# Scores for the maxima of attention: from six products of parts in one set of TensorE's rows to three products in two sets

## The chip, the cores and the metric

The kernel runs on one core of a Trainium2 chip. A core has TensorE (PE; its weight loads are shown as PEld), VectorE (DVE), ScalarE (ACT), GpSimd (POOL) and SyncE (SP), which only issues transfers here. The metric is the device time of one execution in microseconds, taken as the median of the runs.

## What is computed

One pre-norm transformer layer on x of shape (2, 2048, 256), in float32. The attention has 16 heads of 16 features, with rotation by position and a causal mask:

```python
q, k = (rope(q), rope(k))
att = jnp.einsum('bhqd,bhkd->bhqk', q, k) / scale
att = jnp.where(mask, att, -jnp.inf)
att = jax.nn.softmax(att, axis=-1)
y = jnp.einsum('bhqk,bhkd->bhqd', att, v)
```

The feed-forward part has 704 inner features; each of its three products takes both operands rounded blockwise (16 numbers share a scale) to the FP4 grid and scaled back:

```python
gate = fp4_linear(x, w_gate)
y = fp4_linear(x, w_up)
h = jax.nn.silu(gate) * y
return fp4_linear(h, w_down)
```

Each half is x plus its result on the normalised x.

## The kernel before, in words

**Tiling.** The 4096 rows are 8 chunks of 512 queries (four for each of the two sequences), and the heads are four groups of four. A chunk and a group make a unit: 32 units (`units`), worked in order. c is the number of chunks before the unit's own in its sequence, 0 to 3.

**Parts.** q and k are split into three bf16 numbers each (high, middle, low), stored to `parts_dram`, and dealt from there by SyncE into `q_mem` and `k_mem` (`deal`, L804 to L826, three DMAs each for q and k of a unit). The dealing lays the parts above each other in the rows (partitions) so that one product over 96 rows, `TERM_ROWS`, adds six products of parts of 16 features: float32 accuracy from bf16. Three more rows of q hold the negative maximum in parts and meet ones in k.

**Maxima.** For a stable softmax each query's largest score is found first (`maxima`, L864 to L879 on TensorE, L1268 to L1283 on VectorE). A piece is 32 queries of the four heads by 512 keys: four matmuls, each over 96 rows into its own 32 columns of the array, side by side, fill one bank of PSUM. VectorE takes the maximum of each row: of past keys by a reduction (L1282), of the unit's own chunk by an operation that adds the triangular mask and takes the maximum (L1279, shown as a custom operation and a read of the accumulator). Own blocks have 32, 64, ... 512 keys, two in a bank where they fit. In all there are 1056 pieces (768 of them past), at most `S_IN_FLIGHT` = 3 undrained.

**Placing.** After the last piece of a unit VectorE forms the negative maxima in three parts and turns them; three DMAs (`place_maxima`, L725 to L732) put them into rows of `q_mem`, by ScalarE's queue for the first two chunks and by SyncE's later.

**Probabilities.** For each of a unit's key tiles (128 keys) and each head, four matmuls of 32 keys each (L896, rows 0 to 98) give scores less the maximum; at the diagonal four more add the mask (L901). ScalarE takes the exponential into `prob` (L1177). Then four float32 matmuls, one a head, add prob times V to bank 7 (`values`, L920; each is recorded as two).

**The rest.** Projections (L966 to L999), a tile's feed-forward part in units of 128 queries (L927 to L1044), normalising (L1006) and the weights' turning use the whole array. Rounding to the grid takes six steps on VectorE and three on GpSimd (`quantise`, L1492 to L1505): add, subtract, and multiply by the scale, each on the whole row of 256 or 704 numbers.

**Order.** A planner at the head of `preln_layer` (`Plan`, `rehearse_...`) rehearses all jobs with assumed durations before the kernel is written. It takes the job that can start first; among those that could start at once, the one that was ready first, less the ns in `SOONER_NS`. A job that keeps TensorE's present division (divided into tiles or whole) counts as ready `BESIDE_NS` = 2500 ns sooner, and a change of division is put down with `DIVIDE_NS` = 96 or `JOIN_NS` = 150. The order found is the program order of each engine and of each queue, fixed; seven banks of PSUM are given out by the same plan.

Of the kernel before, what the change touches and what calls it, by code (L numbers as in the profile page):

```python
# [21 lines left out]
RUNS = ((0, 3), (3, 2), (5, 1))  # L22
TERM_ROWS = sum(terms for _, terms in RUNS) * HD
ROWS = TERM_ROWS + SPLIT
GROUP = 4

COLUMNS = 32
# [14 lines left out]
S_IN_FLIGHT, ST_IN_FLIGHT = 3, 3  # L42
# [5 lines left out]
DMA_TURN_NS, DMA_NS, DMA_KB_PER_NS, DIVIDE_NS, JOIN_NS, BESIDE_NS = 460, 1500, 0.2, 96, 150, 2500  # L48
SOONER_NS = dict(a=0, w=0, xn=10000, s=200, st=0, pv=-1000, place=10000, norm=200, c=(0, -2000), tile=1000)
# [24 lines left out]
class Plan:  # L74
# [5 lines left out]
    def __init__(self, banks):  # L80
# [4 lines left out]
        self.divided, self.sharing = False, (0.0, 0.0)  # L85

    def start(self, job, sooner=0.0):

        self.jobs.append([self.now, sooner, job, (None, [], None, False), 0.0])

    def wait(self, names=(), until=None):
        yield None, list(names), until, False

    def load(self, queue, name, kbytes, after=()):

        yield queue, list(after), None, False
        self.move(queue, name, kbytes, after)
# [6 lines left out]
    def step(self, engine, name, ns, after=(), shares=False, divided=False):  # L104


        yield engine, list(after), None, divided
        self.do(engine, name, ns, after, shares, divided)

    def do(self, engine, name, ns, after=(), shares=False, divided=False):  # L110
        if engine == "pe" and divided != self.divided:
            ns, self.divided = ns + (DIVIDE_NS if divided else JOIN_NS), divided
# [11 lines left out]
        self.end[name] = begin + ns + HANDOVER_NS[engine]  # L124

    def through(self, use, ns, engine, drain_ns, after=(), drain_after=(), first=None, divided=False):

        yield "pe", list(after), lambda: self.spare, divided
# [6 lines left out]
        self.do("pe", use, ns, [*after, free], divided=divided)  # L135
# [27 lines left out]
    def goes(self, job):  # L163
        ready = self.ready(job)
        sooner = job[1]() if callable(job[1]) else job[1]
        if job[3][0] == "pe" and self.divided == job[3][3]:
            sooner += BESIDE_NS
        return max(ready, self.engine_free.get(job[3][0], 0.0)), ready - sooner
# [16 lines left out]
def preln_layer(nc, x, Wq, bq, Wk, bk, Wv, bv, Wo, bo, w_gate, w_up, w_down,  # L185
# [35 lines left out]
    BLOCKS = CHUNK // COLUMNS  # L221
    pieces, final_piece = [], {}
    for u, (k, g) in enumerate(units):
        c = k % NCHUNKS
        pieces += [(u, [(0, n, j * BANK, BANK, j, False)]) for n in range(BLOCKS) for j in range(c)]
        for n in range(BLOCKS // 2):
            of = [n, BLOCKS - 2 - n] if 2 * n < BLOCKS - 2 else [n]
            widths = [(n_ + 1) * COLUMNS for n_ in of]
            pieces.append((u, [(sum(widths[:m]), n_, c * BANK, widths[m], c, True) for m, n_ in enumerate(of)]))
        pieces.append((u, [(0, BLOCKS - 1, c * BANK, BANK, c, True)]))  # L230
# [113 lines left out]
    def rehearse_key_ones():  # L344
        for c in range(NCHUNKS):
            yield from plan.wait(until=lambda: not spare_users[c])
            yield from plan.load("sp", ("key ones", c), 48)
# [4 lines left out]
    def rehearse_deals():  # L352
        for u, (k, g) in enumerate(units):
# [4 lines left out]
            for n, (_, terms) in enumerate(RUNS):  # L358
                yield from plan.load("sp", ("deal q", u, n), 64 * terms, free)
            free = stored + ([("st", GROUP * final_step[(NCHUNKS - 1) * NGROUPS + g] + 3)] if k >= NCHUNKS else [])  # L360
            for n, (_, terms) in enumerate(RUNS):
                yield from plan.load("sp", ("deal k", u, n), 64 * terms, free)

    def rehearse_maxima():
        for n, (u, parts) in enumerate(pieces):
            keys, own = sum(part[3] for part in parts), parts[0][5]
            yield from plan.wait([("deal q", u, len(RUNS) - 1)] + ([("deal k", u, len(RUNS) - 1)] if own else [])
                                 + ([("place", u - 2, 2)] if u >= 2 else [])
# [1239 lines left out]
```

## Time and profile before

| what | value |
|---|---|
| median of 3 runs | 1302.66 us (1300.41 to 1303.75) |
| profiled execution, its own time | 1298.29 us |
| its span, first to last instruction | 1296.5 us |
| granted clock of TensorE, mean | 0.983 of full speed |
| TensorE matmuls busy | 1219.2 us |
| VectorE busy | 1097.2 us |
| ScalarE busy | 763.1 us |
| GpSimd busy | 470.5 us |

The profile is of one execution. "Busy" is the union of an engine's instruction records. Ends of matmuls are modelled, and neighbours overlap; what a matmul costs the queue is read from the start of one to the start of the next. In a row of the order of time the first number is the start in us, the second the length of the merged group; "x4" is the count of instructions. In a row of line groups there follow the busy time of the group, the mean ns of one, and the idle time before it with what ended it.

### The profile page before, as it was taken

The page shows a single profiled execution, that of the slowest core. Times are in us where ns is not written, and L with a number is a line of the kernel's source. Part 1 is how long each engine was busy: PE and PEld are TensorE (multiplying, and loading weights), DVE is VectorE, ACT ScalarE, POOL GpSimd, SP SyncE. Part 2 cuts the span into 40 slices and gives each one's busy share as a digit, 9 for nine tenths or more (in the row PEclk, how much of TensorE's full clock was granted, in tenths as well). Part 3 has the DMA queues.
Part 4 walks back from the last instruction along what each step waited for, and adds up shares of the span by engine and source line. Part 5 has one row for each costly group of instructions (what it writes and reads, how often), then busy time and mean ns, then how long its engine had stood idle before and what let it go on. Part 6 is the DMA issues. An engine that isn't in the chain of part 4 may idle for free.

```text
span 1296.5 us, 40306 instructions
## 1 busy us (share of the span) xinstructions
PE 1219.2 (94%) x16886; PEld 689.7 (53%) x16886; DVE 1097.2 (85%) x2946; ACT 763.1 (59%) x1658; POOL 470.5 (36%) x501
## 2 busy tenths in 40 slices
PE   7679999899999999999999999999999999999867
PEld 6445555455555555555466555545545555554345
DVE  5799998889898999979479989899998999985066
ACT  4346776456564676656655655646565675656721
POOL 2944665553221112131445562332221112023145
PEclk9879999899999999999999999999999999999989
DMA  4734222311001101101023222111011100000000
GB/s 105 177 96 118 72 78 62 92 30 43 16 21 38 31 2 43 27 10 36 14 64 91 67 67 60 35 34 39 11 30 35 35 2 19 2 6 14 13 13 17
DMA packets 63937, 57.28 MB, mean 44 GB/s; under 512 B 17534, under 2 KB 57344, under 8 KB 63744
## 3 DMA queue, kind: packets, MB, share of 16 engines
q1 hardware_dynamic: 60728, 53.62, 15.9%
q8 instruction: 133, 2.18, 0.7%
q10 hardware_dynamic: 3028, 1.09, 0.3%
q14 instruction: 48, 0.39, 0.1%
HBM read 37.51 MB, written 16.78 MB: 42 GB/s over the span
## 4 chain that ended last, share of the span: by engine, by line
PE 70%; DVE 16%; ACT 6%; issue 3%; POOL 2%; DMA 2%; ACTq 1%; SPq 0%; DVEq 0%; POOLq 0%
PE bank L920 14%; PE bank L932 14%; PE bank L875 13%; PE bank L896 12%; PE bank L1044 7%; DVE bank L1279 6%; ACT prob L1177 5%; DVE piece_max L1282 4%; PE bank L991 4%; PE bank L1035 2%; PE bank L999 2%; PE bank L927 1%; DVE piece_max L1279 1%; PE bank L1006 1%; PE bank L901 1%
## 5 line engine op out<-in xcount | busy, mean ns | idle before, releaser
L1177 ACT ACTIVATE prob<-bank 128x512 f32<-128x512 f32 (+3 forms) x1280 | 594.5, 542 | 280.2 <-PE bank L896 172.6
L1282 DVE TENSOR_REDUCE piece_max<-bank 128x1 f32<-128x512 f32 x768 | 488.1, 676 | 7.1 <-PE bank L875 6.1
L896 PE MATMUL bank<-q_mem,k_mem 99*32 99x512 bf16 (+13 forms) x5120 | 383.9, 341 | 10.6 <-DMA q_mem<-max_rows 8.1
L875 PE MATMUL bank<-k_mem,q_mem 96*32 96x512 bf16 (+14 forms) x5120 | 381.5, 344 | 9.3 <-DVE piece_max L1279 5.5
L920 PE MATMUL bank<-prob,V 128*32 128x512 f32 (+3 forms) x2560 | 293.8, 531 | 15.6 <-ACT prob L1177 11.9
L1496 POOL TENSOR_TENSOR c_mem<-c_mem 128x256 f32<-128x256 f32 (+2 forms) x74 | 85.0, 1149 | 420.3 <-DVE c_mem L1370 420.3
L875 PEld LDWEIGHTS bank<-k_mem,q_mem 96*32 96x32 bf16 x5120 | 135.4, 96 | 182.8 <-issue 104.1
L896 PEld LDWEIGHTS bank<-q_mem,k_mem 99*32 99x32 bf16 x5120 | 145.3, 96 | 152.9 <-issue 65.4
L1279 DVE CUSTOM_DVE_ANT_0 bank<-bank,past_keys 128x32 f32<-128x32 f32 (+15 forms) x512 | 207.9, 468 | 2.8 <-PE bank L875 2.5
L920 PEld LDWEIGHTS bank<-prob,V 128*32 128x32 f32 x2560 | 70.6, 110 | 67.3 <-ACT prob L1177 30.0
L901 PE MATMUL bank<-mask_kq,ident_h 128*32 128x128 bf16 (+3 forms) x2048 | 100.7, 200 | 0.0
L1499 POOL TENSOR_TENSOR c_mem<-c_mem 128x256 f32<-128x256 f32 (+2 forms) x74 | 86.6, 1171 | 4.9
L1044 PE MATMUL bank<-WdT,c_mem 128*128 128x256 f32 x360 | 86.7, 391 | 1.1 <-ACT c_mem L1217 0.8
L932 PE MATMUL bank<-WgT,c_mem 128*128 128x352 f32 x240 | 84.1, 474 | 0.5 <-ACT c_mem L1204 0.5
L932 PE MATMUL bank<-WuT,c_mem 128*128 128x352 f32 x240 | 80.7, 460 | 0.2 <-ACT prob L1177 0.2
L1210 ACT ACTIVATE c_mem<-bank 128x352 f32<-128x352 f32 x60 | 27.9, 465 | 84.6 <-PE bank L932 77.5
L1044 PEld LDWEIGHTS bank<-WdT,c_mem 128*128 128x128 f32 x360 | 67.5, 193 | 19.1 <-issue 8.5
L1502 POOL TENSOR_TENSOR c_mem<-c_mem 128x256 f32<-128x256 f32 (+2 forms) x74 | 71.4, 966 | 4.5
L1486 POOL TENSOR_SCALAR c_mem<-c_mem 128x1 f32<-128x1 f32 x30 | 6.9, 231 | 178.5 <-DVE c_mem L1339 178.5
L901 PEld LDWEIGHTS bank<-mask_kq,ident_h 128*32 128x32 bf16 x2048 | 57.8, 97 | 25.1 <-issue 8.9
L1279 DVE DVE_READ_ACCUMULATOR2_ANT piece_max<- 128x1 f32 x512 | 70.2, 137 | 0.0
L1448 DVE SCALAR_TENSOR_TENSOR c_mem<-c_mem,bank 128x352 f32<-128x352 f32 x60 | 31.0, 516 | 40.0 <-ACT c_mem L1210 39.7
(173 smaller groups left out, 1394.5 us busy)
## 6 DMA issues: line engine op xcount, KB each, us to landing
parts_dram<-a_mem SPq DMA_DIRECT2D x13, 512.0 KB, 3.5
q_mem<-parts_dram SPq DMA_DIRECT2D x32, 192.0 KB, 2.9
k_mem<-parts_dram SPq DMA_DIRECT2D x32, 192.0 KB, 3.5
q_mem<-parts_dram SPq DMA_DIRECT2D x32, 128.0 KB, 3.0
k_mem<-parts_dram SPq DMA_DIRECT2D x32, 128.0 KB, 3.5
c_mem<-in_L_attn_x SPq DMA_DIRECT2D x30, 128.0 KB, 2.1
out<-c_mem SPq DMA_DIRECT2D x30, 128.0 KB, 1.7
a_mem<-in_L_attn_x SPq DMA_DIRECT2D x13, 256.0 KB, 2.8
```

The lines of the kernel that those rows point to most:

```text
L875: m = pe.matmul(b[COLUMNS * h:COLUMNS * (h + 1), of], q_rows(u)[0:TERM_ROWS, h, block * COLUMNS:(block + 1) * COLUMNS], k_rows(k0 // CHUNK ...
L896: mm = pe.matmul(b[k0:k0 + COLUMNS, since:CHUNK], k_rows(j // TPC, g)[:, h, first:first + COLUMNS], q_rows(u)[:, h, since:CHUNK], start=Tr ...
L901: mm = pe.matmul(b[k0:k0 + COLUMNS, off:off + k0 + COLUMNS], ident_h[:, k0:k0 + COLUMNS], mask_kq[:, 0:k0 + COLUMNS], start=False, stop=Tr ...
L920: mm = pe.matmul(O[COLUMNS * h:COLUMNS * (h + 1), off:CHUNK], V[:, of % V_SLOTS, j % TPC, v0:v0 + 32], prob[:, (GROUP * m + h) % NP, off:C ...
L932: m = pe.matmul(b[:, 0:width], src[:, d * P:(d + 1) * P], w[:, d, lo:lo + width], start=(d == 0), stop=(d == DK - 1))
L1044: m = pe.matmul(b[:, 0:D], hT[0:DOWN[j], j * P:(j + 1) * P], WdT[0:DOWN[j], j, :], start=(j == 0), stop=(j == len(DOWN) - 1))
L1177: act.activation(prob[:, n % NP, off:CHUNK], bank_of("st", n)[:, off:CHUNK], ACT.Exp, scale=SCALE).then_inc(drained("st", n)[0], 1)
L1279: r = dve.tensor_tensor_reduce(scores, scores, past_keys[:, BANK - keys:BANK], scale=1.0, scalar=LOWEST, op0=ALU.add, op1=ALU.max, accum_o ...
L1282: r = dve.tensor_reduce(most, scores, AX.X, ALU.max)
L1496: pool.tensor_tensor(a, a, b, ALU.add).then_inc(done, 1)
L1499: pool.tensor_tensor(a, a, b, ALU.subtract).then_inc(done, 1)
L1502: pool.tensor_tensor(dst.rearrange("p (n f) -> p n f", f=FP4_BLOCK), a.rearrange("p (n f) -> p n f", f=FP4_BLOCK), v["scale"][0:rows, 0:nb ...
```

## The change

- Of the six products of parts the maxima take only the three largest: high by high, high by middle and middle by high. They fill 48 rows. The even heads' three lie in rows 0 to 47 and the odd heads' in rows 64 to 111 (`RUNS`, `UPPER_ROWS`); the three smaller products lie in the other half of the rows. Rows 48 to 63 are zeros, loaded once, and the maxima's rows are 112 to 114. The probabilities still take all, over 115 rows.
- A piece is now two even or two odd heads by 64 queries by 512 keys, in one bank; an even piece uses rows 0 to 47, its odd partner rows 64 to 111. There are 768 past pieces as before and 320 own ones, in pairs.
- Own blocks are masked on TensorE by four matmuls more for each part of a piece; VectorE has one plain reduction for every part.
- The dealing takes six DMAs for q and six for k (even and odd heads apart), keys of chunk 0 by ScalarE's queue; placing takes six.
- The planner knows three divisions: whole, by columns (probabilities, sums with V) and by rows (maxima). Staying counts 500 ns in the two divided ones and nothing in the whole one. `S_IN_FLIGHT` and `ST_IN_FLIGHT` are 4, and `SOONER_NS["c"]` is (1000, 500) instead of (0, -2000).
- GpSimd's three rounding steps on 704 numbers are done as six on 352.

The core of the diff:

```diff
-RUNS = ((0, 3), (3, 2), (5, 1))
+RUNS = ((64, 0, 3), (0, 64, 2), (32, 96, 1))
+UPPER_ROWS = 3 * HD
-S_IN_FLIGHT, ST_IN_FLIGHT = 3, 3
+S_IN_FLIGHT, ST_IN_FLIGHT = 4, 4
+BESIDE_NS = dict(whole=0, columns=500, rows=500)
...
+        if engine == "pe" and tile[0] == BY_ROWS:
+
+            self.engine_free["pe"], self.rows_free[tile[1]] = begin + ISSUE_NS, max(self.rows_free + [begin + ns])
...
-                        for h in range(GROUP):
-                            m = pe.matmul(b[COLUMNS * h:COLUMNS * (h + 1), of],
-                                          q_rows(u)[0:TERM_ROWS, h, block * COLUMNS:(block + 1) * COLUMNS],
-                                          k_rows(k0 // CHUNK, g)[0:TERM_ROWS, h, k0 % CHUNK:k0 % CHUNK + keys],
-                                          start=True, stop=True)
+                        for tile in range(GROUP):
+                            at32, head = tile // 2 * COLUMNS, 2 * (tile % 2) + odd
+                            of = keys - COLUMNS + at32 if own else keys
+                            m = pe.matmul(b[COLUMNS * tile:COLUMNS * (tile + 1), column:column + of],
+                                          q_rows(u)[rows, head, block * BLOCK + at32:block * BLOCK + at32 + COLUMNS],
+                                          k_heads(k0 // CHUNK, g)[rows, head, k0 % CHUNK:k0 % CHUNK + of],
+                                          start=True, stop=not own, skip_group_check=own)
+                        for tile in range(GROUP if own else 0):
+                            at32 = tile // 2 * COLUMNS
+                            m = pe.matmul(b[COLUMNS * tile:COLUMNS * (tile + 1), column + keys - BLOCK + at32:column + keys],
+                                          ident_h[half, HALF_ROWS * odd:HALF_ROWS * odd + COLUMNS],
+                                          mask_qk[half, 0:BLOCK - at32], start=False, stop=True, skip_group_check=True)
...
-                        if own:
-                            at.wait_ge(ones_made, 4)
-                            at.wait_ge(mask_loaded[0], 16 * GROUP)
-                            r = dve.tensor_tensor_reduce(scores, scores, past_keys[:, BANK - keys:BANK], scale=1.0, scalar=LOWEST,
-                                                         op0=ALU.add, op1=ALU.max, accum_out=most)
-                        else:
-                            r = dve.tensor_reduce(most, scores, AX.X, ALU.max)
+                        r = dve.tensor_reduce(piece_max[:, u % 2, n_, slot:slot + 1],
+                                              bank_of("s1", n)[:, column:column + keys], AX.X, ALU.max)
...
+                for n, half in itertools.product(range(3), range(halves)):
+                    at_, of = slice(half * each, (half + 1) * each), slice(half * nb, (half + 1) * nb)
```

## Rows read from the trace of the kernel before

**Rows 1.** The page's busy times: engine, us, share of the span, instructions.
```profile
PE 1219.2 (94%) x16886; PEld 689.7 (53%) x16886; DVE 1097.2 (85%) x2946; ACT 763.1 (59%) x1658; POOL 470.5 (36%) x501
```

**Rows 2.** Busy time by stretch: its us, then busy us (instructions) of each engine.
```profile
core 0: us, PE busy (x) PEld busy (x) DVE busy (x) ACT busy (x) POOL busy (x), PEclk, DMA share, GB/s
60.00:200.00 140.00, 125.59 (x2182) 70.38 (x2186) 134.70 (x449) 88.74 (x202) 81.46 (x85) 0.93 0.34 89
...
400.00:600.00 200.00, 199.39 (x2989) 106.90 (x2991) 184.74 (x494) 127.61 (x270) 43.11 (x48) 1.00 0.09 22
```

**Rows 3.** The chain that ended last, share of the span by engine.
```profile
PE 70%; DVE 16%; ACT 6%; issue 3%; POOL 2%; DMA 2%; ACTq 1%; SPq 0%; DVEq 0%; POOLq 0%
```

**Rows 4.** The order of time on TensorE from 907.66 us.
```profile
907.66 0.39 PE L875 MATMUL bank<-k_mem,q_mem 96*32 96x512 bf16 x4
907.88 0.39 PE L896 MATMUL bank<-q_mem,k_mem 99*32 99x512 bf16 x4
908.10 0.39 PE L875 MATMUL bank<-k_mem,q_mem 96*32 96x512 bf16 x4
908.31 0.39 PE L896 MATMUL bank<-q_mem,k_mem 99*32 99x512 bf16 x4
908.63 0.44 PE L927 MATMUL bank<-ident,c_mem 128*128 128x128 f32 x2
...
909.22 0.61 PE L875 MATMUL bank<-k_mem,q_mem 96*32 96x512 bf16 x8
909.66 0.60 PE L920 MATMUL bank<-prob,V 128*32 128x512 f32 x4
```

**Rows 5.** The page's group of the maxima's matmuls.
```profile
L875 PE MATMUL bank<-k_mem,q_mem 96*32 96x512 bf16 (+14 forms) x5120 | 381.5, 344 | 9.3 <-DVE piece_max L1279 5.5
```

**Rows 6.** The order of time on TensorE, around changes of division.
```profile
901.38 2.86 PE L1044 MATMUL bank<-WdT,c_mem 128*128 128x256 f32 x12
...
299.66 0.38 PE L1044 MATMUL bank<-WdT,c_mem 96*128 96x256 f32 x1
299.97 0.39 PE L896 MATMUL bank<-q_mem,k_mem 99*32 99x512 bf16 x4
```

**Rows 7.** VectorE's maxima: groups of the page, by form, and ten in order of time.
```profile
L1282 DVE TENSOR_REDUCE piece_max<-bank 128x1 f32<-128x512 f32 x768 | 488.1, 676 | 7.1 <-PE bank L875 6.1
L1279 DVE CUSTOM_DVE_ANT_0 bank<-bank,past_keys 128x32 f32<-128x32 f32 (+15 forms) x512 | 207.9, 468 | 2.8 <-PE bank L875 2.5
L1279 DVE DVE_READ_ACCUMULATOR2_ANT piece_max<- 128x1 f32 x512 | 70.2, 137 | 0.0
L1279 DVE CUSTOM_DVE_ANT_0 bank<-bank,past_keys 128x512 f32<-128x512 f32 x32 | 22.9, 716 | 0.0
L1279 DVE CUSTOM_DVE_ANT_0 bank<-bank,past_keys 128x288 f32<-128x288 f32 x32 | 15.8, 494 | 0.0
1049.36 6.11 DVE L1282 TENSOR_REDUCE piece_max<-bank 128x1 f32<-128x512 f32 x10 [0.25 <-PE bank L875]
```

**Rows 8.** The order of time on TensorE, masked pieces of the probabilities.
```profile
300.22 0.38 PE L896 MATMUL bank<-q_mem,k_mem 99*32 99x480 bf16 x4
300.40 0.22 PE L901 MATMUL bank<-mask_kq,ident_h 128*32 128x128 bf16 x4
300.45 0.39 PE L896 MATMUL bank<-q_mem,k_mem 99*32 99x480 bf16 x4
```

**Rows 9.** The order of time on SyncE's queue: dealing q of one unit.
```profile
899.83 1.26 SPq L815 DMA_DIRECT2D q_mem<-parts_dram  x3
```

**Rows 10.** TensorE's waits: us in total, times, longest us.
```profile
PE bank L896 <- DMA q_mem<-max_rows: 8.1, 5, 2.4
PE bank L927 <- POOL c_mem L1502: 7.0, 1, 7.0
```

**Rows 11.** GpSimd's second rounding step, by form.
```profile
L1499 POOL TENSOR_TENSOR c_mem<-c_mem 128x704 f32<-128x704 f32 x32 | 54.0, 1688 | 2.3
L1499 POOL TENSOR_TENSOR c_mem<-c_mem 128x256 f32<-128x256 f32 x40 | 31.2, 781 | 2.5
```

More of the change, by code:

```diff
@@ L1 @@
+import itertools
 from contextlib import ExitStack
@@ L102, in move, with step, tensor_free, do @@
         self.end[name] = self.moved + DMA_NS
[L104 to L112, printed above, removed]
+    def step(self, engine, name, ns, after=(), shares=False, tile=(WHOLE, None)):
+        yield engine, list(after), None, tile
+        self.do(engine, name, ns, after, shares, tile)
+    def tensor_free(self, tile):
+        division, half = tile
+        free = self.engine_free.get("pe", 0.0)
+        if division == BY_ROWS and self.division == BY_ROWS:
+            return max(free, self.rows_free[half])
+        return max([free] + self.rows_free)
+    def do(self, engine, name, ns, after=(), shares=False, tile=(WHOLE, None)):
+        if engine == "pe":
+            self.engine_free["pe"] = self.tensor_free(tile)
+            if tile[0] != self.division:
+                ns, self.division = ns + (JOIN_NS if tile[0] == WHOLE else DIVIDE_NS), tile[0]
         since = self.running[4] if self.running else 0.0
@@ L134, in through @@
         self.end[free] = self.bank_free[b]
-        self.do("pe", use, ns, [*after, free], divided=divided)
+        self.do("pe", use, ns, [*after, free], tile=tile)
         self.start(self.drain(use, b, engine, drain_ns, drain_after, first), self.running[1])
@@ L165, in goes @@
         sooner = job[1]() if callable(job[1]) else job[1]
-        if job[3][0] == "pe" and self.divided == job[3][3]:
-            sooner += BESIDE_NS
-        return max(ready, self.engine_free.get(job[3][0], 0.0)), ready - sooner
+        free = self.engine_free.get(job[3][0], 0.0)
+        if job[3][0] == "pe":
+            free = self.tensor_free(job[3][3])
+            if self.division == job[3][3][0]:
+                sooner += BESIDE_NS[self.division]
+        return max(ready, free), ready - sooner
     def run(self, over=lambda: False):
@@ L346, in rehearse_key_ones @@
             yield from plan.wait(until=lambda: not spare_users[c])
+            yield from plan.load("sp", ("key zeros", c), 256)
             yield from plan.load("sp", ("key ones", c), 48)
@@ L385, in rehearse_placing @@
         free = [("st", GROUP * final_step[u - Q_SLOTS] + 3)] if u >= Q_SLOTS else []
[L386 to L387 removed]
+        for n in range(2 * SPLIT):
+            yield from plan.load("act" if placed_by_scalar(u) else "sp", ("place", u, n), 2, [("neg5", u)] + free)
     def rehearse_probabilities():
@@ L424, in rehearse_rounding @@
             last = [("round", n) + key]
-        for n in range(3):
-            yield from plan.step("pool", ("grid", n) + key, 150 + (2.1 if n < 2 else 1.7) * width, last)
-            last = [("grid", n) + key]
+        halves = grid_halves(width)
+        for n, half in itertools.product(range(3), range(halves)):
+            yield from plan.step("pool", ("grid", n, half) + key, 150 + (2.1 if n < 2 else 1.7) * width / halves,
+                                 [("grid", n - 1, half) + key] if n else last)
     def rehearse_weight_loads():
@@ L1268, in maxima @@
             def maxima():
-                for n, (u, parts) in enumerate(pieces):
+                for n, (u, odd, parts) in enumerate(pieces):
                     yield when["drain", "s1", n]
```

305 lines of the change are left out of this document (171 added, 134 removed).

## The prediction

> **What bounds the kernel now.** I read the busy times first, then the busy times by stretch, then the chain that ended last, the waits of TensorE, and last the order of time on TensorE. By the busy times TensorE's matmuls fill 94% of the span and VectorE 85%, GpSimd 36% [rows 1]. By stretch the picture splits in two: from 60 to 200 us VectorE is busy 134.7 of 140 us and TensorE 125.6, so VectorE leads there; from 400 to 600 us TensorE is busy 199.4 of 200 us and VectorE 184.7 [rows 2]. The chain agrees: 70% of it is TensorE, 16% VectorE [rows 3]. So most of the span is a backlog on TensorE, with VectorE seldom more than a tenth behind it. A change pays if it takes time out of TensorE's queue, and a saving on VectorE pays mostly before 200 us.
>
> What a matmul costs is read in the order of time, since the records' ends overlap. A piece of scores for the maxima (L875, four matmuls side by side on 32 columns each, 512 keys) starts 0.22 us before what follows it (907.66, 907.88, 908.10) [rows 4], though its records last 344 ns on average [rows 5]. A change between this divided array and the whole array costs more: from 908.31 to 908.63 it is 0.32 us where 0.22 is usual [rows 4]. The other way, a matmul of L1044 ordinarily holds the next one up by (2.86 - 0.40) / 11 = 0.22 us in a row of twelve, but 0.31 us where a divided piece follows (299.66 to 299.97) [rows 6]. So one change of division costs about 0.095 us, either way.
>
> **The change, part by part.**
>
> *Maxima in two sets of rows.* There are 768 pieces of 512 past keys, and for each of the 32 units an own chunk of eight pieces' worth of 512 columns and one of 256. At 0.219 us for 512 columns that is 768 x 0.219 = 168 us and 32 x 8.5 x 0.219 = 59.5 us, 227 us in all; L875's records cover 381.5 us, but they overlap those of others [rows 5]. Afterwards an even and an odd piece (two heads by 64 queries each) can stream at the same time through rows 0 to 47 and 64 to 111: 384 x 0.219 = 84 us and 32 x 4.5 x 0.219 = 31.5 us (blocks of 64 queries waste a bit more of the triangle), 115.5 us if every piece has its partner. Full pairing saves 112 us. A piece that runs alone gives its half back. VectorE frees one bank each 0.61 us (ten reductions in 6.11 us) [rows 7], so the partner's bank comes free up to 0.61 us after the first's; TensorE's backlog, and the plan's 500 ns in favour of the division that is set, let both be ready in most cases. I take nine in ten paired: 112 less 0.1 x 115.5, about 101 us saved. Bounds: 54 us (half paired) and 112.
>
> *Masks on TensorE.* 256 pairs of own parts get four more matmuls of 64 or 32 columns per tile. The nearest rows are the masked pieces of the probabilities: from 299.97 to 300.22 [rows 6, 8] it is 0.25 us and from 300.22 to 300.45 [rows 8] 0.23 us, against 0.22 us unmasked. That is 0.01 to 0.03 us each, and for narrow parts I allow the same again: 256 x 0.03 = 8 us. Bounds 3 and 25 us.
>
> *A third division of the array.* Before, maxima, probabilities and sums with V share one division, so they alternate free of cost: at 907.66, 907.88, 908.10, 908.31 they take turns piece by piece [rows 4]. Afterwards every turn from rows to columns and back is a change of division. The trace has no such change; the nearest is that between divided and whole, 0.095 us, and I see no reason for another size. Bounds 0.05 and 0.15 us. How many there are is the number that decides. In [rows 4] four pieces make three bursts, 1.3 pieces each. Now in one burst there can be up to four (four may be in flight, before three), the pair comes together by nature, and the 500 ns bonus holds a burst together. I take 2.8 pieces a burst: 1088 / 2.8 = 389 bursts, 778 borders. [rows 4] show one block of whole-array work to four pieces; over the run I estimate one to seven (some five blocks for each of 32 tiles), so about 155 of these borders fall on one that is paid today: 623 x 0.095 = 59 us.
>
> The Trainium skill (TensorEngine Tiling (Array Packing), Key Properties) says that changing the tiling mode, not only the tile, drains the TensorE; that speaks against this part of the change, and 0.32 against 0.22 us shows such a drain between whole and divided; no row shows it between rows and columns. The same page says that different tiles work in parallel.
>
> *VectorE.* The masked own maxima are a custom operation of 468 ns on average plus a readout of 137 ns, 512 times: 310 us of records. A plain reduction of 512 columns is 676 ns; the custom one goes from 716 ns at 512 to 494 at 288 [rows 7], so 0.99 ns a column, and a plain one at 288, the new mean, should take about 454: 512 x 454 = 232 us. VectorE loses 78 us. Most of it is no time of the kernel, for TensorE sets the pace. Seven of the 32 units have their own chunks in the stretch to 200 us, 17 us of the 78. Bounds: 0, and 25 us if VectorE's share of the chain [rows 3] shrinks in proportion over the whole run. I take 12.
>
> *Dealing, placing, zeros.* SyncE issues a unit's q parts in three DMAs, 1.26 us [rows 9]; now there are six for q and six for k, and six placings instead of three, each 0.42 us. SyncE carries 2.5 us more for a unit, against 16 to 50 us that a unit lasts; the tiles' loads and stores queue behind it and have that slack. The placing is on the path where a unit's first probabilities wait for it: 8.1 us in 5 waits today [rows 10]. Three further issues make each 1.3 us longer: 3 us in all. Cover gone, over all units, it would be 40 us. The first chunk's keys go by ScalarE's queue: 24 issues there, beside probabilities that have hardly begun.
>
> *GpSimd by halves.* A step on 704 numbers takes 1688 ns, on 256 numbers 781 ns [rows 11]: 2.02 ns a number and 263 ns fixed. Two halves cost 263 ns more a step, 0.79 us more a row of three steps, 25 us of GpSimd over 32 rows of tiles and weights, on an engine that is idle for two thirds. It hurts where TensorE waits for L1502 (7.0 us, one wait) [rows 10]: 3 us. A gain by shorter blockings of VectorE is possible, up to 10 us; I take none.
>
> *Sum:* -101 + 8 + 59 - 12 + 3 + 3 = -40 us. The profiled execution took 1298.29 us (span 1296.5 and 1.8 around it), so 1258 us for it. The median of the runs shown is 1302.66, 4.4 above the profiled one: **1263 us**.
>
> **The rivals.**
> - *Bursts of four, all paired.* 272 bursts, 544 borders, less 155: 37 us. -112 + 8 + 37 - 25 = -92 us: 1211 us. For it speaks that VectorE has up to 2.4 us of work in four banks, so TensorE may come late; against it, that today even three in flight are rarely taken at once [rows 4].
> - *It cancels.* Bursts of two, eight in ten paired: 89 us of changes against 89 saved, +8 - 12 + 6: +2 us, 1305 us. The Trainium skill (TensorEngine Tiling (Array Packing), PSUM Bottleneck) has a rule of this kind: tiling speeds up the matmuls but not the emptying of PSUM. Here VectorE's 0.61 us for a bank stays as it is, so what TensorE gains comes back as waits for banks, and it would end at about this time.
> - *Slower: the pairs break.* If VectorE's one bank per 0.61 us sets when a piece may go, TensorE takes each alone: 1.5 pieces a burst, half of them paired, 1451 borders less 155, 123 us of changes, and 54 saved: +77 - 12 + 6 = +71, 1374 us. It decides below some two pieces a burst; there changes cost more than pairing brings. For it speaks the 1.3 of today, against it the bonus of 500 ns and the four in flight.
> - *It doesn't do what it says:* the two sets of rows don't stream together. Then the maxima keep 227 us and the changes are paid on top: 4 + 8 + 59 - 12 + 6 = +65, 1368 us. Against it: on columns four tiles do run together, 4 matmuls in 0.22 us.
>
> **How the numbers follow.** The forecast's case has a chance of 0.50, bursts of four 0.17, cancelled 0.12, broken pairs 0.17, no overlap 0.04. The forecast's own range is 1235 to 1288 us. For 8 in 10 it goes down to 1212, which takes in half of the case of long bursts, and up to 1330, which takes in the cancelled case and the milder half of broken pairs. Within 0.3% (4 us), about what a measurement of this kernel can tell from no change, lie 0.06, from the cancelled case; faster 0.50 + 0.17 + 0.04 = 0.71; slower 0.17 + 0.04 + 0.02 = 0.23.
>
> **What would show it.** Right: in the order of time, an odd piece starts within 0.03 us of its even one, and the next work 0.22 us later, plus 0.1 at a border; the maxima's bursts hold 8 to 12 matmuls and more; VectorE's busy time near 1020 us with no custom operation; TensorE still above 90%. Wrong: bursts of 4 matmuls; a row of TensorE's waits in which VectorE's reductions stand with tens of us (a partner waits for its bank); placings above 20 us among the waits; a border that costs clearly more or less than 0.095 us.

## The result, and the profile of the changed kernel

The changed kernel takes **1338.65 us** (1333.43 to 1341.41); the kernel before, beside it, 1303.2. The ratio is **1.0248**, 95% interval 1.0213 to 1.0283: slower, and outside the range that was given.

The page's busy times of the changed kernel, and its chain by engine:

```profile
PE 1248.3 (93%) x18934; PEld 624.0 (47%) x18934; DVE 1077.8 (80%) x2434; ACT 760.5 (57%) x1660; POOL 489.1 (37%) x602
...
PE 75%; ACT 8%; DVE 7%; DMA 3%; SPq 3%; issue 2%; ACTq 1%; POOL 1%; POOLq 0%; DVEq 0%
```

TensorE is busy 29 us more than in [rows 1], and the span is 43 us longer. VectorE's share of the chain has fallen from 16% [rows 3] to 7%, but SyncE's queue, 0% there, now holds 3%. The order of time on TensorE shows that what the change says, it does:

```profile
1041.50 0.52 PE L948 MATMUL bank<-k_mem,q_mem 48*32 48x512 bf16 x8
1041.95 1.06 PE L997 MATMUL bank<-prob,V 128*32 128x512 f32 x8
1042.94 0.41 PE L948 MATMUL bank<-k_mem,q_mem 48*32 48x512 bf16 x8
1043.28 1.05 PE L973 MATMUL bank<-q_mem,k_mem 115*32 115x512 bf16 x16
```

Eight matmuls of maxima, two pieces, hold the next work up by 0.34 us (1042.94 to 1043.28). Less 0.095 for the change of division that is 0.245 us, where one piece alone took 0.22 [rows 4]. The two sets of rows stream together. They do so for most pieces: in the 422 bursts of the maxima, 138 of the 1280 parts (four matmuls each, two small parts sharing a bank) are left over without a partner, 11% where one in ten was forecast.

**Where the 43 us are.** The table adds up, over all matmul records of a trace, the time from one start to the next. 0.095 us is taken out at each change of division; idle time is what lies between a record's modelled end and the next start, where it is above 0.03 us; of the time at half the clock, half is put down to the clock. The rest is the work itself. Times in us, one profiled execution each; the columns after the second are experiments, told below.

| | before | changed | b_48_rows | a_same_order_columns | b_place_six | a_place_two | b_place_one |
|---|---|---|---|---|---|---|---|
| maxima, bare | 240.1 | 168.8 | 240.4 | 255.0 | 240.3 | 168.4 | 239.2 |
| all other matmuls, bare | 934.0 | 949.0 | 937.7 | 946.1 | 931.8 | 949.4 | 931.6 |
| changes of division (number) | 30.6 (322) | 99.8 (1051) | 169.5 (1784) | 40.1 (422) | 30.6 (322) | 99.8 (1051) | 30.6 (322) |
| half clock | 14.0 | 30.3 | 33.8 | 16.1 | 32.2 | 18.0 | 15.8 |
| idle | 69.1 | 82.7 | 55.3 | 81.3 | 94.0 | 73.4 | 64.5 |
| first to last start | 1287.8 | 1330.7 | 1436.6 | 1338.6 | 1328.9 | 1309.0 | 1281.7 |

From before to changed: maxima -71, changes of division +69, other work +15, half clock +16, idle +14. What pairing gives, the changes of division take back to 2 us; the loss is in the rest.

The row of the half clock has to be read with care, for it differs from one execution of a kernel to the next. The profiled execution of before was a quick one (1298.29 us, mean clock 0.983), that of the changed kernel the longest of its four (1341.41 us, 0.966). That is why the table has 43 us where the medians have 35. In the experiments below 13 executions of before had 0.970 to 0.979, median 0.975, against 0.9675 for the changed kernel; the share of the clock that is missing, times the time, is 33 and 43 us. So the half clock makes 10 us of the difference at most (an estimate from these clocks), not 16. A kernel that differs from before only in GpSimd's halves (experiment 6, 2 us slower) has 25.9 us in this row.

The largest single wait is at the start. The order of time there, on VectorE, ScalarE's queue and TensorE of the changed kernel:

```profile
79.08 0.23 DVE L1389 STREAM_TRANSPOSE max_rows<-max_parts 128x64 bf16<-128x64 bf16 x1
79.34 4.95 ACTq L784 DMA_DIRECT2D q_mem<-max_rows  x6
...
81.66 0.27 PE L954 MATMUL bank<-mask_qk,ident_h 64*32 64x64 bf16 x4
92.66 0.61 PE L973 MATMUL bank<-q_mem,k_mem 115*32 115x512 bf16 x4 [10.72 <-DMA q_mem<-max_rows]
```

and of the kernel before:

```profile
72.47 0.23 DVE L1311 STREAM_TRANSPOSE max_rows<-max_parts 128x64 bf16<-128x64 bf16 x1
72.73 1.83 ACTq L732 DMA_DIRECT2D q_mem<-max_rows  x3
...
76.22 0.61 PE L896 MATMUL bank<-q_mem,k_mem 99*32 99x512 bf16 x4 [2.09 <-DMA q_mem<-max_rows]
```

From the maxima in rows to the first probabilities it took 3.75 us and takes 13.6. TensorE stands still for 10.7 of them, and its clock is low around it. Three more issues are the smaller part of the difference. The chain in order of time shows the last transfer of the unit, from its issue to its landing, in the changed kernel and in the kernel before:

```profile
83.03 9.59 DMA q_mem<-max_rows
```
```profile
73.95 2.23 DMA q_mem<-max_rows
```

Counted from the turned maxima, the sixth transfer is issued 2.5 us later than the third was, and it then takes 7.4 us more to land. SyncE's queue had begun to issue loads of zeros, weights and x at 82.18 us; that these hold the landing up is likely but not shown. By stretch, the changed kernel from 56 to 97 us and the kernel before from 60 to 80:

```profile
56.00:97.00 41.00, 18.22 (x428) 8.69 (x432) 26.92 (x70) 9.33 (x15) 19.75 (x19) 0.50 0.60 140
```
```profile
60.00:80.00 20.00, 10.56 (x143) 3.87 (x147) 20.00 (x82) 5.34 (x8) 12.37 (x11) 0.50 0.45 119
```

The granted clock is 0.50, that is 1.2 of 2.4 GHz, for 41 us instead of 20.

### The profile page after: what moved, and what is told of

Same layout as the page of the kernel before. It is cut to its first block, busy times and chain, and to the rows that moved or that the text cites. A ratio compares the mean times of both kernels' runs of the same rounds, so it can differ in the third digit from the quotient of the medians.

```text
span 1339.6 us, 44312 instructions
## 1 busy us (share of the span) xinstructions
PE 1248.3 (93%) x18934; PEld 624.0 (47%) x18934; DVE 1077.8 (80%) x2434; ACT 760.5 (57%) x1660; POOL 489.1 (37%) x602
## 4 chain that ended last, share of the span: by engine, by line
PE 75%; ACT 8%; DVE 7%; DMA 3%; SPq 3%; issue 2%; ACTq 1%; POOL 1%; POOLq 0%; DVEq 0%
PE bank L997 16%; PE bank L973 15%; PE bank L1009 13%; PE bank L948 12%; ACT prob L1259 7%; PE bank L1121 6%; PE bank L1068 4%; DVE piece_max L1359 3%; PE bank L1112 2%; PE bank L1076 2%; PE bank L1004 1%; ACTq L784 1%; PE bank L1083 1%; PE bank L978 1%; DMA q_mem<-max_rows 1%
## 5 line engine op out<-in xcount | busy, mean ns | idle before, releaser
L1359 DVE TENSOR_REDUCE piece_max<-bank 128x1 f32<-128x512 f32 (+7 forms) x1280 | 684.4, 583 | 63.3 <-PE bank L948 32.9
L973 PE MATMUL bank<-q_mem,k_mem 115*32 115x512 bf16 (+12 forms) x5120 | 340.7, 347 | 23.9 <-DMA q_mem<-max_rows 12.4
L948 PE MATMUL bank<-k_mem,q_mem 48*32 48x512 bf16 (+15 forms) x5120 | 241.2, 349 | 18.5 <-DMA q_mem<-parts_dram 5.7
L973 PEld LDWEIGHTS bank<-q_mem,k_mem 115*32 115x32 bf16 x5120 | 128.4, 96 | 221.8 <-issue 101.4
L1581 POOL TENSOR_TENSOR c_mem<-c_mem 128x352 f32<-128x352 f32 (+1 forms) x106 | 89.4, 857 | 251.1 <-DVE c_mem L1448 251.1
L948 PEld LDWEIGHTS bank<-k_mem,q_mem 48*32 48x32 bf16 x5120 | 84.9, 91 | 203.2 <-issue 128.8
L978 PE MATMUL bank<-mask_kq,ident_h 128*32 128x96 bf16 (+3 forms) x2048 | 97.0, 202 | 0.0
L1630 POOL TENSOR_TENSOR c_mem<-c_mem,out_bias 128x256 f32<-128x256 f32 x30 | 21.7, 730 | 200.1 <-DMA c_mem<-in_L_attn_x 200.0
L1584 POOL TENSOR_TENSOR c_mem<-c_mem 128x352 f32<-128x352 f32 (+1 forms) x106 | 91.0, 872 | 2.4
L997 PEld LDWEIGHTS bank<-prob,V 128*32 128x32 f32 x2560 | 61.2, 110 | 64.2 <-issue 30.9
L1292 ACT ACTIVATE c_mem<-bank 128x352 f32<-128x352 f32 x60 | 27.9, 465 | 92.7 <-PE bank L1009 83.1
L1587 POOL TENSOR_TENSOR c_mem<-c_mem 128x352 f32<-128x352 f32 (+1 forms) x106 | 78.0, 749 | 2.3
L954 PE MATMUL bank<-mask_qk,ident_h 64*32 64x64 bf16 (+1 forms) x2048 | 71.4, 190 | 0.0
```

What stands on the lines that cost most here:

```text
L948: m = pe.matmul(b[COLUMNS * tile:COLUMNS * (tile + 1), column:column + of], q_rows(u)[rows, head, block * BLOCK + at32:block * BLOCK + at3 ...
L954: m = pe.matmul(b[COLUMNS * tile:COLUMNS * (tile + 1), column + keys - BLOCK + at32:column + keys], ident_h[half, HALF_ROWS * odd:HALF_ROW ...
L973: mm = pe.matmul(b[k0:k0 + COLUMNS, since:CHUNK], k_heads(j // TPC, g)[0:ROWS, h, first:first + COLUMNS], q_rows(u)[0:ROWS, h, since:CHUNK ...
L978: mm = pe.matmul(b[k0:k0 + COLUMNS, off:off + k0 + COLUMNS], ident_h[:, k0:k0 + COLUMNS], mask_kq[:, 0:k0 + COLUMNS], start=False, stop=Tr ...
L997: mm = pe.matmul(O[COLUMNS * h:COLUMNS * (h + 1), off:CHUNK], V[:, of % V_SLOTS, j % TPC, v0:v0 + 32], prob[:, (GROUP * m + h) % NP, off:C ...
L1359: r = dve.tensor_reduce(piece_max[:, u % 2, n_, slot:slot + 1], bank_of("s1", n)[:, column:column + keys], AX.X, ALU.max)
```

## The experiments

Names with a are built on the changed kernel, names with b on the kernel before. All ratios are to the kernel before in the same comparison, whose median was 1307 to 1308 us there. The changed kernel was not timed again beside them: differences to it are taken from its 1338.65 us, and from the ratios they come out up to 2 us otherwise.

**1. What does a change of division cost?** The kernel before, in its own order, with the maxima on 48 rows:

```diff
-RUNS = ((0, 3), (3, 2), (5, 1))
+RUNS = ((3, 3), (0, 2), (2, 1))
...
-                                          q_rows(u)[0:TERM_ROWS, h, block * COLUMNS:(block + 1) * COLUMNS],
-                                          k_rows(k0 // CHUNK, g)[0:TERM_ROWS, h, k0 % CHUNK:k0 % CHUNK + keys],
+                                          q_rows(u)[0:LARGEST, h, block * COLUMNS:(block + 1) * COLUMNS],
+                                          k_rows(k0 // CHUNK, g)[0:LARGEST, h, k0 % CHUNK:k0 % CHUNK + keys],
```

`LARGEST` is 48.

> The kernel before, order and instructions unchanged, but the maxima multiply only rows 0 to 47, where the three largest products now lie, so TensorE works them in a division by rows, one piece at a time. Theory 'changes of division': each turn between maxima and probabilities or sums now costs the 0.095 us that the trace of the changed kernel shows at every border; the trace of before has about 1570 such turns, so 1570 x 0.095 = 149 us more: 1430 to 1455 us. Rival 'changes are free or hidden, the loss is elsewhere (dealing, start)': within 10 us of before, 1303 us.

Measured: 1446.35 us, ratio 1.1058 (1.1024 to 1.1092), 138 us more, as the first theory had it. The order of time on its TensorE:

```profile
1002.47 0.40 PE L876 MATMUL bank<-k_mem,q_mem 48*32 48x512 bf16 x4
1002.79 0.83 PE L897 MATMUL bank<-q_mem,k_mem 99*32 99x512 bf16 x12
1003.55 0.40 PE L876 MATMUL bank<-k_mem,q_mem 48*32 48x512 bf16 x4
1003.88 0.32 PE L921 MATMUL bank<-prob,V 128*32 128x128 f32 x4
```

The same piece of four matmuls holds the next work up by 0.32 to 0.33 us (1002.47 to 1002.79, 1003.55 to 1003.88) instead of 0.22 [rows 4]. The trace has 1462 changes more, 139 us at 0.095; in the table 14 us less of idle time and 20 us more of half clock stand beside them. The price between rows and columns is about the price between divided and whole, and nothing covers it. The rival is out.

**2. Do pairing and changes cancel?** The changed kernel in its own order, every piece over all six products:

```diff
-                    rows = slice(HALF_ROWS * odd, HALF_ROWS * odd + UPPER_ROWS)
+                    rows = slice(0, MAX_ROW)
...
-                                          ident_h[half, HALF_ROWS * odd:HALF_ROWS * odd + COLUMNS],
-                                          mask_qk[half, 0:BLOCK - at32], start=False, stop=True, skip_group_check=True)
+                                          ident_h[:, HALF_ROWS * odd:HALF_ROWS * odd + COLUMNS],
+                                          mask_qk[:, 0:BLOCK - at32], start=False, stop=True, skip_group_check=True)
```

> The changed kernel with its order kept, but every piece of the maxima multiplies rows 0 to 111 (all six products) in the division by columns, so no two pieces stream together and the 629 turns between rows and columns vanish. Theory 'both are real and nearly cancel': the maxima cost TensorE some 100 us more (their bare time is 169 us, nearly all in pairs), the changes 629 x 0.095 = 60 us less: +40, about 1378 us. Rival 'the two sets of rows do not really stream together': only the 60 us are saved, about 1279 us.

Measured: 1354.01 us, 1.0348 (1.0314 to 1.0381): 15 us slower than the changed kernel. The table: maxima +86, changes -60, half clock -14. So the sets of rows are worth 15 us in this order, less than the 40 expected, since the maxima lose 86 and not 100. The profiled executions differ by 8 us only, for the half clock of the changed kernel's was high. The rival (1279 us) is out.

**3. What do the masks cost on TensorE?** The changed kernel, each of the maxima's mask matmuls twice:

```diff
-                        for tile in range(GROUP if own else 0):
+                        for repeat, tile in itertools.product(range(2), range(GROUP if own else 0)):
```

> The changed kernel with each of the maxima's mask matmuls issued twice (2048 matmuls and weight loads more). Theory 'masks cost TensorE 28 us, not 8': about +25 to +30, 1366 us. Rival 'masks cost 8 us as predicted, the rest of the own parts' excess is their uneven widths': +8, 1347 us.

Measured: 1349.77 us, 1.0323 (1.0282 to 1.0364). That is 11 us more than the changed kernel, between the two expectations; in its trace the maxima's bare time is 183.8 us, 15 more. The masks cost about 15 us, not 8 and not 28. What else the own parts take above their columns is left open.

**4. Is VectorE's relief worth anything?** The kernel before in its order, own blocks masked on TensorE by four matmuls of 32 columns and reduced plainly:

```diff
-                            r = dve.tensor_tensor_reduce(scores, scores, past_keys[:, BANK - keys:BANK], scale=1.0, scalar=LOWEST,
-                                                         op0=ALU.add, op1=ALU.max, accum_out=most)
...
+                        for h in range(GROUP if own else 0):
+                            m = pe.matmul(b[COLUMNS * h:COLUMNS * (h + 1), column + keys - COLUMNS:column + keys],
+                                          ident_h[:, 0:COLUMNS], mask_qk[:, :], start=False, stop=True, skip_group_check=True)
```

> The kernel before, order unchanged, with the own maxima masked by four matmuls of 32 columns more on TensorE and a plain reduction on VectorE. Theory 'TensorE sets the pace': TensorE gets 512 x 0.03 to 0.05 = 15 to 25 us more, VectorE 78 us less, the kernel 5 to 20 us slower, 1308 to 1323 us. Rival 'VectorE's relief pays': 10 to 25 us faster, 1278 to 1293 us.

Measured: 1309.48 us, 1.0017 (1.0000 to 1.0034): 2 us more, less than the one theory had and not the gain of the other. Its busy times:

```profile
PE 1228.8 (94%) x18934; PEld 708.8 (54%) x18934; DVE 1085.7 (83%) x2434; ACT 763.6 (58%) x1659; POOL 470.4 (36%) x500
```

TensorE is busy 9.6 us more and VectorE only 11.5 us less than in [rows 1]. The records of VectorE's maxima overlap: in the trace of before they sum to 829 us and cover 698, in this one 741 and 677. So a difference of 88 us in the sum of lengths is one of 22 us in what they cover, and the prediction took the sum of lengths. That the relief is worth nothing does not follow, though. Counted as in the table, the maxima take 251.4 us of TensorE here instead of 240.1, 11 us more, and the kernel is 2 us slower. If TensorE's 11 us came out as in experiment 1 (in full) or 3 (11 of 15 us), the relief gave back some 7 to 10 us on the kernel before. This is an estimate; no run has the one without the other.

**5. Dealing and placing.** The kernel before in its order, with the dealing in twelve transfers a unit and the placing in six (`b_deals_split`), then each alone, and the dealing once more with heads 0 and 1, 2 and 3 together. The placing's edit:

```diff
-                engine.dma_start(q_rows(u)[TERM_ROWS + p:TERM_ROWS + p + 1].rearrange("o h t -> o (h t)"),
-                                 max_rows[p % 2:P:2, u % 2, p // 2, :]).then_inc(max_placed[u % 2], 16)
+                for b in range(2):
+                    engine.dma_start(q_rows(u)[TERM_ROWS + p:TERM_ROWS + p + 1, 2 * b:2 * b + 2].rearrange("o h t -> o (h t)"),
+                                     max_rows[64 * b + p % 2:64 * (b + 1):2, u % 2, p // 2, :]).then_inc(max_placed[u % 2], 16)
```

and the dealing's, for q:

```diff
-                    sp.dma_start(q_rows(u)[first * HD:(first + terms) * HD].rearrange("p h t -> p (h t)"),
-                                 src).then_inc(q_dealt[u % Q_SLOTS], 16)
+                    for odd in range(2):
+                        sp.dma_start(q_rows(u)[first * HD:(first + terms) * HD, odd:GROUP:2, :],
+                                     src[:, g * GROUP + odd:(g + 1) * GROUP:2]).then_inc(q_dealt[u % Q_SLOTS], 16)
```

> The kernel before, its order of jobs unchanged, with q and k dealt in twelve DMAs a unit instead of six (even and odd heads apart) and the maxima placed in six instead of three. Theory 'the start of the changed kernel is late because of its dealing and placing': the first probabilities, at 76.2 us before and 92.7 us in the changed kernel, come 8 to 15 us later, and the kernel takes 8 to 20 us more, 1312 to 1325 us. Rival 'transfers are hidden here too, the late start comes from the order of the new plan': within 4 us of before.

> The kernel before, order unchanged, with only the placing of the maxima split into six transfers of 2 KB instead of three of 4 KB. Theory 'the placing': its issues of about 0.6 us each lie between the maxima's end and the first probabilities of a unit, 1.8 us more for each of 32 units where TensorE has nothing else queued before them; most of the 36 us of the kernel with both splits, 20 us or more. Rival 'the dealing': at most 8 us.

> The kernel before, order unchanged, with only the dealing split into twelve transfers a unit (even and odd heads apart, runs of 1 KB). Theory 'the dealing': SyncE's queue carries six issues more for a unit, and placings, loads and stores queue behind them: 20 us or more of the 36. Rival 'the placing': at most 10 us.

> As the twelve transfers a unit on the kernel before, but heads 0 and 1 in one and heads 2 and 3 in the other, so that every run of memory is 2 KB instead of 1 KB. Theory 'number of issues': the same time as with even and odd heads apart, within 4 us. Rival 'short runs': it comes back by half or more towards the kernel before.

| kernel | us | ratio (interval) |
|---|---|---|
| both splits | 1343.69 | 1.0294 (1.0252 to 1.0337) |
| placing in six | 1336.54 | 1.0210 (1.0176 to 1.0243) |
| dealing in twelve, runs of 1 KB | 1320.65 | 1.0098 (1.0072 to 1.0124) |
| dealing in twelve, runs of 2 KB | 1321.68 | 1.0095 (1.0073 to 1.0116) |

Placing the same 12 KB of a unit in three transfers more costs 28 us, with not one matmul added; six transfers of dealing more cost 13 us, with runs of either length. It is the number of transfers, not their bytes or their runs. Both together cost 36 us, as much as the whole change and more than the 8 to 20 that were expected. They did it otherwise than expected: the first probabilities come 2.8 us later (79.0 instead of 76.2 us), not 8 to 15, so the splits don't account for the late start of the changed kernel (92.7 us). The chain and TensorE's wait of the kernel with six placings, and its placings on SyncE's and ScalarE's queue (count: duration in ns, min/median/max):

```profile
PE 60%; DVE 23%; ACT 5%; issue 3%; DMA 3%; SPq 3%; ACTq 2%; POOL 1%; POOLq 0%; DVEq 0%
...
PE bank L897 <- DMA q_mem<-max_rows: 22.6, 12, 5.0
...
L733 SPq DMA_DIRECT2D q_mem<-max_rows x144: 457/594/1572, 277.4 to 1205.4; - x144
L733 ACTq DMA_DIRECT2D q_mem<-max_rows x48: 464/616/1939, 72.5 to 230.0; - x48
```

A placing takes its queue 0.6 us, not the 0.42 of a dealing [rows 9]. The loss builds up over many units, mostly early: the same probabilities start 20 us later than in the trace of before at 198 us, 28 us later at 314 and 39 us at the end. TensorE waits 22.6 us in 12 waits where it was 8.1 in 5 [rows 10], and from 60 to 200 us it is busy less and granted less:

```profile
60.00:200.00 140.00, 116.95 (x1908) 66.18 (x1908) 121.84 (x408) 75.62 (x173) 67.70 (x76) 0.85 0.32 82
```

against 125.59 us at 0.93 in [rows 2]. The table has both, idle +25 and half clock +18 us, 41 us in all where the medians differ by 28. By the clocks of all executions of this comparison (medians 0.975 and 0.9675) the half clock makes 11 us at most. With the dealing in twelve the chain shows the queue again:

```profile
PE 71%; DVE 11%; ACT 5%; SPq 5%; DMA 3%; issue 3%; POOL 2%; ACTq 0%; POOLq 0%; DVEq 0%
```

**6. GpSimd by halves alone,** on the kernel before, in its order; each of the three steps on 704 numbers is issued as two on 352.

```diff
+                    for half in range(halves):
+                        at_, of = slice(half * each, (half + 1) * each), slice(half * nb, (half + 1) * nb)
```

> The kernel before, order unchanged, with GpSimd's three rounding steps on 704 numbers done as six on 352. Theory of the prediction: GpSimd gets 25 us of work more, the kernel 0 to 5 us slower. Rival: VectorE is blocked for a shorter time by each step, VectorE's busy time falls by several us and the kernel by up to 5 us.

Measured: 1309.58 us, 1.0025 (1.0002 to 1.0048), 2 us slower, as the prediction had it. The rival is out.

**7. Placing by two queues,** on the changed kernel:

```diff
-                    *(place_maxima(sp, at, u) for u in range(len(units)) if not placed_by_scalar(u)),
+                    *(place_maxima(sp, at, u, range(1, 2 * SPLIT, 2) if placed_by_scalar(u) else range(2 * SPLIT)) for u in range(len(units))),
```

> The changed kernel, order of jobs unchanged, with three of the six placings of each unit of the first two chunks issued by SyncE and three by ScalarE, instead of all six by ScalarE. Theory 'the wait of 10.7 us for the first placing is the queue of six issues': the first probabilities start 4 to 8 us earlier than 92.7 us, TensorE's half clock from 56 to 97 us ends sooner, the kernel is 5 to 12 us faster. Rival 'packets of other transfers hold the placing up, not its issues': no change beyond 3 us.

Measured: 1333.69 us, 1.0204 (1.0167 to 1.0242), 5 us faster, within the intervals of both. The first probabilities start at 93.6 us, not 4 to 8 us before 92.7, after a wait of 11.1 us. The experiment doesn't part theory and rival: SyncE issues its three between its own loads, at 83.1, 84.3 and 87.5 us, so the last goes out 4.5 us later than the sixth did on ScalarE's queue (83.0), and lands 6.0 us after that. What slows the landing at the start is left open.

**8. Fewer changes by a new order:** 2500 ns instead of 500 in favour of the division that is set.

```diff
-BESIDE_NS = dict(whole=0, columns=500, rows=500)
+BESIDE_NS = dict(whole=0, columns=2500, rows=2500)
```

> The changed kernel planned anew with 2500 ns instead of 500 in favour of the division that is set; the order found has 869 changes of division instead of 1051. Theory 'only the number of changes matters': 182 x 0.095 = 17 us faster, 1321 us. Rival 'holding TensorE in one division starves ScalarE and VectorE': TensorE's idle time grows by more than the 17 us and the kernel is slower than 1338 us.

Measured: 1395.77 us, 1.0667 (1.0616 to 1.0718). The changes fall by 182 or 17 us, but the kernel is slower, as the rival had it: idle time grows from 82.7 to 128.5 us and the half clock's part from 30.3 to 55.6. Half of the idle time that is new is waits for the placing, 35.3 us in 17 instead of 12.4 in 3. The number of changes alone is no aim.

**9. Fewer placings.** The number subtracted from a query's scores cancels in the quotient of the softmax, so it needs no float32 accuracy: its high bf16 part will do. Middle and low part, their rows, and three short steps of VectorE are left out. On the kernel before one transfer remains, on the changed one two.

```diff
-ROWS = TERM_ROWS + SPLIT
+ROWS = TERM_ROWS + 1
...
-            for p in range(SPLIT):
+            for p in range(1):
...
-                yield when["neg2", u]
-                at.wait_ge(done, first + 2)
-                dve.tensor_tensor(rest, whole, high, ALU.subtract).then_inc(done, 1)
```

> The changed kernel, order unchanged, with only the high part (bf16) of each negative maximum placed, by two transfers instead of six, and three short steps of VectorE less a unit; left out are the middle and the low part, and rows 113 and 114. Any number near the maximum serves, since it cancels in the quotient. Theory 'the six placings make most of the changed kernel's loss': 20 to 35 us faster, 1304 to 1319 us. Rival 'the plan has hidden them, the changes of division and the masks make the loss': within 8 us of 1338.

> The same, with the planner told of it (a new order, 1042 changes of division). Theory 'placings': 1295 to 1315 us. Rival 'changes of division': 1325 us or more.

> The kernel before, order unchanged, with only the high part of each negative maximum placed, by one transfer instead of three, and three short steps of VectorE less; the middle and low part and their rows are left out, which cancels in the quotient. Theory 'every placing is on the path by about 0.3 us a unit as with six': 28 x 2 / 3 = 19 us faster, 1285 to 1293 us. Rival 'three are covered, only more than three stick out': 0 to 8 us faster.

> The same kernel with the planner told of it. Theory: as in the order given or a few us better, 1280 to 1293 us. Rival: within 8 us of before.

| kernel | us | ratio (interval) |
|---|---|---|
| changed, two placings, same order | 1319.29 | 1.0090 (1.0064 to 1.0116) |
| changed, two placings, planned anew | 1321.42 | 1.0109 (1.0075 to 1.0142) |
| before, one placing, same order | 1295.85 | 0.9908 (0.9879 to 0.9937) |
| before, one placing, planned anew | 1311.75 | 1.0031 (1.0014 to 1.0047) |

The changed kernel gets 19 us of its 35 back, with the same 1051 changes; in the table half clock -12 and idle -9. Three things went at once, four of six transfers, two thirds of the bytes and three short steps of VectorE, and these runs don't part them. TensorE's waits for the placing, 12.4 us before this edit, become 3.6, but another takes their place:

```profile
PE bank L973 <- DVE piece_max L1359: 11.8, 7, 9.5
...
PE bank L973 <- DMA q_mem<-max_rows: 3.6, 1, 3.6
```

The first probabilities start at 80.6 instead of 92.7 us. Five pieces on TensorE stands still for 9.5 us, and the sixth starts at 92.5 instead of 94.9; the clock is low for 41 us as before. Behind VectorE's reductions the chain in order of time has a load, for which VectorE stood still 10.6 us:

```profile
82.44 8.32 DMA a_mem<-in_L_attn_x
```

So 2.4 of the 19 us are won in that stretch, 11.7 by 235 us, and the rest later, 4.9 of it between 497 and 672 us.

The kernel before gets 12 us faster and **beats both kernels, at 1295.85 us**. It gains less than the 19 expected and more than the 8 of the rival. In its trace 6.1 us are won by the first probabilities (70.1 instead of 76.2 us) and 2.8 in all the rest (the two traces differ by 8.9), so after the start three placings were mostly covered, while the loss with six went on growing. The new orders, expected at 1295 to 1315 and at 1280 to 1293 us, were no better, in one case 16 us worse than the old: the planner's assumed durations do not rank orders that finely.

## Why the prediction was wrong, point by point

- **What bounds the kernel: right.** TensorE's backlog. Experiment 1 put 139 us into its queue, and 138 came out.
- **The sum by its terms.** The forecast was -40 us and +35 came, 75 us away. The maxima with their masks are off by 22 us, the changes of division by 10, the other matmuls' 15 stood in no term, and the transfers are off by up to 33, as they cost on the kernel before. These add up to 80; they are taken from different kernels, so the fit is a rough one.
- **Price of a change of division, 0.095 us: right,** though taken from another pair of divisions. **Their number: nearly.** 623 more were forecast and 729 came. The maxima's bursts, 422 against 389, add 66 of the 106; the rest is that the whole-array work stands in 211 blocks instead of 161. 69 us instead of 59.
- **Maxima in pairs: right in kind, too large.** 93 us net of masks were forecast and 71 came (the maxima before are 240 us by the table, not 227, and 169 after, not 134). Masks are 15 us instead of 8 (experiment 3). A pair takes 0.245 us instead of 0.219, which over 384 pairs of past pieces is 10 us. Some 5 us are open. So the two large terms, forecast at -34 us together, gave -2. This is the rival "it cancels", by the numbers of the sum and not by waits for banks: the maxima wait 4.8 us for VectorE's reductions, 5.5 before (the largest part of the idle time in [rows 5]).
- **VectorE, -12 us: its working was wrong, its size is open.** VectorE's busy time fell 19 us (1097.2 to 1077.8), not 78, for the term was worked out from record lengths that overlap. Masks moved to TensorE bring nothing in all (experiment 4); by the estimate there the relief alone was worth some 7 to 10 us on the kernel before, so that the term may have been near by luck.
- **Dealing and placing, +3 us: the step that failed.** It priced the placing by the waits of TensorE in the trace of before, 1.3 us for each of the waits seen, and gave all other units their cover. (Five waits at 1.3 us are 6.5 us; the sum has 3.) To the dealing's six issues more it gave no time at all. It also named 40 us as the price with the cover gone, and left that out of the range. On the kernel before the splits cost 36 us, 28 by the placing alone: waits for it became 12 where 5 were seen, so the cover that the trace of before showed was gone with three issues more. In the changed kernel two placings instead of six give 19 us back. How much of the changed kernel's loss the twelve dealings make, in its own order, was not measured; on the kernel before it is 13 us. Whether the new order of jobs costs something by itself was not measured either. A part of the mistake is the clock: with six placings the time at half the clock grew with the idle time, by 11 us at most.
- **GpSimd, +3 us: right** (2 us).
- **"Slower: the pairs break" was the wrong rival.** It was slower for another reason; the pairs held. The 15 us by which all other matmuls' bare time grew in the changed kernel (and in every experiment on it, 946 to 950 against 930 to 938) are shown by the table. About 5 of them are sums with V: 236.5 us before, 241.1 in the changed kernel, 241.2 with experiment 1's division by rows, and 236.8 again in experiment 2, where that division is gone. So a change there costs a little over 0.095 us. For the other 10 no run names the cause.

## What to carry to other kernels

Count the transfers that stand between two stages, not their bytes: each is 0.6 us of issue here, on a path that the busy times don't show, and a trace in which few waits stick out doesn't say that one more is covered. When such a wait goes, look at what TensorE waits for next. When two halves of an array are set against a second division of it, multiply the number of turns by 0.095 us first; here they ate all but 2 us of the gain. A number that cancels in the result needs no exact parts, and leaving them out gained 12 us where the change lost 35.

## What the runs showed of the hardware

- A change of division costs about 0.1 us whichever two of the three divisions it joins: the piece of four matmuls holds the next work up by 0.32 us at a border and 0.22 within. The Trainium skill (TensorEngine Tiling (Array Packing), Key Properties) says that a change of the tiling mode drains TensorE; these 0.10 us at a border agree with it.
- Two pieces in two sets of rows take 0.245 us together, 0.22 us one alone.
- The clock was lower where transfers made TensorE idle more: in the 140 us from 60 us on it was 0.93 with three placings (0.91 in experiment 6's kernel, which also has three) and 0.85 with six. It also fell, and stayed low, where TensorE was idle for short times only. In the kernel with single pieces on 48 rows, by stretch:

```profile
230.00:260.00 30.00, 27.62 (x404) 12.94 (x400) 23.64 (x59) 16.50 (x36) 16.44 (x15) 1.00 0.24 67
260.00:290.70 30.70, 29.76 (x178) 10.53 (x177) 23.88 (x62) 12.62 (x22) 10.73 (x16) 0.50 0.14 40
```

TensorE was busy 27.6 of the 30 us before the fall to 1.2 GHz, and 7.8 of the last 10, its longest wait there 1.68 us. The clock then stayed at 1.2 GHz for 30.7 us, of which TensorE was busy 29.8. No run explains that.
